# A two-stage graph network on one core: where the edge lists stand in SyncE's queue, and at which block of the first tile they are turned

## The reference, cut to what matters

```python
x = _layernorm(x + L0_gnn(x, edge_index, edge_type_2, ...))     # R-GCN, 2 relations, D_FF 286
x = _layernorm(x + L1_gnn(x, edge_index, ...))                  # 3 residual graph layers, 256 wide

def L0_gnn(h, edge_index, edge_type, ln_w, W_rel, W_root, bias, wo):
    xn = ln_w * (h * rsqrt(mean(h**2) + 1e-6))
    out = xn @ W_root + bias
    for r in range(2):
        w = (edge_type == r)
        sums = segment_sum(xn[src] @ W_rel[r] * w[:, None], dst)
        out = out + sums / maximum(segment_sum(w, dst), 1.0)[:, None]
    return h + elu(out) @ wo
```

## Time and profile before

| what | value |
|---|---|
| median of 3 runs | 584.37 us (583.69 to 584.87) |
| the profiled execution's own time | 585.49 us |
| its span | 583.7 us (so 1.79 us lie around the span) |
| TensorE busy | 97% of the span |
| VectorE, ScalarE, GpSimd busy | 65%, 40%, 17% |
| mean granted TensorE clock | 0.991 |

### The profile page before, as it was taken

The page is one execution under the profiler, slowest core; times in us unless marked ns, Lnnn a source line. Parts: engine busy times, 40 slices in busy tenths (PEclk is TensorE's granted clock), DMA queues, the critical chain, the costliest instruction groups (busy, mean ns, idle before and its releaser), DMA issues.

```text
span 583.7 us, 8611 instructions
## 1 busy us (share of the span) xinstructions
PE 566.7 (97%) x2704; PEld 410.8 (70%) x2704; DVE 380.4 (65%) x980; ACT 231.7 (40%) x477; POOL 100.6 (17%) x80
## 2 busy tenths in 40 slices
PE   6999999999999999999999999999999999999992
PEld 3566666566578898987898888877868867455541
DVE  7599988888837898988512330028748667755455
ACT  5444455533224546463321221013223233366555
POOL 3000000000000000003164512302202230132230
PEclk8999999999999999999999999999999999999997
DMA  8500111111031121129300000600100100021123
GB/s 261 154 26 13 35 35 35 35 35 35 0 89 40 37 62 46 46 71 247 128 20 0 0 0 1 226 1 1 38 1 0 36 0 1 1 71 52 54 70 105
DMA packets 20961, 30.74 MB, mean 53 GB/s; under 512 B 5458, under 2 KB 15404, under 8 KB 20928
## 3 DMA queue, kind: packets, MB, share of 16 engines
q1 hardware_dynamic: 20512, 29.66, 17.1%
q10 hardware_dynamic: 416, 0.67, 0.4%
HBM read 25.20 MB, written 5.12 MB: 52 GB/s over the span
## 4 chain that ended last, share of the span: by engine, by line
PE 92%; DMA 3%; DVE 3%; ACT 1%; SPq 0%; issue 0%; DVEq 0%
PE banks L745 20%; PE banks L949 12%; PE banks L1035 12%; PE banks L868 10%; PE banks L731 5%; PE banks L836 5%; PE banks L971 4%; PE banks L961 4%; PE banks L897 4%; PE banks L899 4%; PE banks L878 3%; PE banks L1025 3%; PE banks L739 1%; PE banks L853 1%; DMA w_all<-in_L_gnn_W_rel 1%; DMA cb_b<-in_L_gnn_conv_bias 1%
## 5 line engine op out<-in xcount | busy, mean ns | idle before, releaser
L745 PE MATMUL banks<-w_all,xnT 128*125 128x429 f32 x320 | 130.4, 532 | 2.3 <-DMA w_all<-in_L_gnn_W_rel 2.3
L745 PEld LDWEIGHTS banks<-w_all,xnT 128*125 128x125 f32 x320 | 54.6, 190 | 32.5 <-issue 29.7
L1198 DVE TENSOR_TENSOR adj<-adj,banks 125x220 f32 x160 | 60.9, 381 | 19.5 <-PE banks L731 17.4
L868 PE MATMUL banks<-hT,w_s 128*128 128x250 f32 x320 | 69.0, 375 | 0.2
L868 PEld LDWEIGHTS banks<-hT,w_s 128*128 128x128 f32 x320 | 60.2, 189 | 8.8 <-issue 1.4
L897 PE MATMUL banks<-y_hi,adj 125*125 125x288 f32 x200 | 55.2, 304 | 0.4 <-issue 0.4
L731 PEld LDWEIGHTS banks<-oh_code,oh_low 125*128 125x128 bf16 x320 | 31.0, 97 | 32.0 <-issue 27.9
L899 PE MATMUL banks<-y_lo,adj 125*125 125x286 f32 x200 | 53.5, 294 | 0.0
L1180 DVE TENSOR_TENSOR oh_code<-iota_c,edge 125x880 bf16<-125x880 f16 x80 | 48.9, 611 | 0.0
L1342 DVE TENSOR_SCALAR hT<-banks,g_c,b_c 128x125 f32<-128x125 f32 x60 | 19.4, 401 | 45.0 <-PE banks L853 45.0
L949 PE MATMUL banks<-adj,h_hi 125*128 125x250 f32 (+1 forms) x180 | 48.3, 367 | 0.1
(11 more groups left out here) (206 smaller groups left out, 896.8 us busy)
## 6 DMA issues: line engine op xcount, KB each, us to landing
xt<-in_x SPq DMA_DIRECT2D x15, 448.0 KB
out_x<-ot SPq DMA_DIRECT2D x9, 448.0 KB
w_s<-in_L_gnn_W SPq DMA_DIRECT2D x5, 512.0 KB, 6.4
xn<-in_x SPq DMA_DIRECT2D x5, 448.0 KB
wd_s<-in_L_gnn_Wd SPq DMA_DIRECT2D x1, 2048.0 KB, 12.1
w_all<-in_L_gnn_W_rel SPq DMA_DIRECT2D x6, 286.0 KB, 6.8
wo_s<-in_L_gnn_wo_weight SPq DMA_DIRECT2D x1, 1024.0 KB, 6.2
w_all<-in_L_gnn_W_root SPq DMA_DIRECT2D x3, 286.0 KB, 6.4
```

Source lines behind the costliest of these rows:

```text
L745: ins = pe.matmul(pb[0:P, 2 + 2 * v + n, 0:FH], xnT[:, u], w_all[:, u, n * FH:(n + 1) * FH], start=(u == 0), stop=(u == KD - 1))
L868: ins = pe.matmul(pb[:, b0 if f == 0 else 4 + f % 2, 0:2 * P], w1_s[:, k, f * 128:(f + 1) * 128], hT[:, k], start=(k == 0), stop=(k == KD ...
L1198: dve.tensor_tensor(cols, cols, window(b, q), ALU.add).then_inc(done, 1)
```

## The change

The three edge-list DMAs leave ScalarE's program and are issued by SP, behind w2 (which ends with the fourth eighth of the weights) and ahead of w3. The bounds are turned in front of block 4 instead of 2, the lows in front of block 5 instead of 4, the codes in front of block 6 instead of 5. Each of the first tile's eight blocks now adds one to a new semaphore, `first_turned`, as ScalarE copies it, and block u on TensorE waits for u + 1 of them. One of the two later warming products goes. `xnT_copied` is raised by two more at the start, so its later counts stay as they were.

```diff
--- before.py
+++ after.py
@@ -231,6 +231,7 @@
             sem(n) for n in ("o_gain", "o_res", "f_sq", "f_mv", "f_sd", "f_rstd", "f_shift", "f_done",
                              "xo_done"))
         tails_set = sem("tails_set")
+        first_turned = sem("first_turned")
         half_done, out_half = sem("half_done"), sem("out_half")
         half_mm, half_res, half_mean, half_sq, half_bias = (sem(n) for n in ("half_mm", "half_res", "half_mean", "half_sq",
                                                                             "half_bias"))
@@ -272,7 +273,12 @@
 
             load_x(0, 0)
             sp.dma_start(lnw8[:], ln_w.rearrange("(k p) -> k p", p=128)).then_inc(lnw_in, 16)
-            for q in range(len(PIECES)):
+            load_w(sp, 0)
+            load_w(sp, 1)
+            load_w(sp, 2)
+            for a, d, done in ((dst_i, dst, dst_in), (src_i, src, src_in), (typ_i, typ, typ_in)):
+                sp.dma_start(a[:], d.rearrange("(g e) -> g e", g=G)).then_inc(done, 16)
+            for q in range(3, len(PIECES)):
                 load_w(sp, q)
             load_x(1, 1)
             with sp.Fori(0, T // 2 - 1) as i:
@@ -418,7 +424,7 @@
 
         @block.scalar
         def _(act):
-            for s in (xnT_copied, y_copied, hT_lo, r1_done, d1_done):
+            for s in (xnT_copied, xnT_copied, xnT_copied, y_copied, hT_lo, r1_done, d1_done):
                 act.sem_inc(s, 1)
             def filled(r, cols, n):
 
@@ -476,15 +482,13 @@
 
             act.wait_ge(small_set, 1)
             act.activation(small1[:, 6:7], eps0[:, 0:1], ACT.Sqrt)
-            for a, d, done in ((dst_i, dst, dst_in), (src_i, src, src_in), (typ_i, typ, typ_in)):
-                act.dma_start(a[:], d.rearrange("(g e) -> g e", g=G)).then_inc(done, 16)
             act.wait_ge(lnw_ps, 1)
             act.copy(lnw[:], pb[:, 4, 480:480 + KD]).then_inc(lnw_set, 1)
             act.wait_ge(lnw_set, 1)
-            act.wait_ge(xnT_ps, 1)
-            weigh(0)
-            act.wait_ge(xnT_ps, 2)
-            weigh(1)
+            for k in range(KD):
+                act.wait_ge(xnT_ps, 1 + k // 4)
+                act.activation(xnT[:, k], pb[:, 6 + k // 4, k % 4 * P:(k % 4 + 1) * P], ACT.Copy,
+                               scale=lnw[:, k:k + 1]).then_inc(first_turned, 1)
             squares(0, 0)
             root_of(0, 0)
             act.wait_ge(small_set, 3)
@@ -785,24 +789,21 @@
             pe.wait_ge(xs_in[0], 32)
             turn(0, 0)
             turn(1, 0)
-            warm(2, 5)
+            warm(1, 5)
             for u in range(KD):
-                if u == 0:
-                    pe.wait_ge(xnT_copied, 1 + 1)
-                if u == 4:
-                    pe.wait_ge(xnT_copied, 1 + 2)
+                pe.wait_ge(first_turned, u + 1)
                 for q, ks in enumerate(PIECES):
                     if u == ks[0]:
                         pe.wait_ge(w_in[q], 48)
-                if u == 2:
+                if u == 4:
                     pe.wait_ge(bounds_ready, 1)
                     for i in range(2 * H):
                         ins = pe.transpose(pb[0:1, 4 + i // H, i % H * G:(i % H + 1) * G], bounds[:, i:i + 1], ident[0:G, 0:G])
                     ins.then_inc(bounds_ps, 1)
-                if u == 4:
+                if u == 5:
                     pe.wait_ge(lows_ready, 1)
                     turn_edges(0, e_low)
-                if u == 5:
+                if u == 6:
                     pe.wait_ge(edges_ready, 1)
                     turn_edges(1, e_code).then_inc(edges_ps, 1)
                 if u == KD - 1:
```

## The result

The changed kernel took 585.63 us (median of 12 executions, 584.69 to 587.77) against 584.71 us for the kernel before beside it (12 executions, 583.53 to 586.15). The ratio is 1.0024 with a 95% interval of 1.0013 to 1.0036. (The ratios are estimates of their own, with these intervals, and differ a little from the ratio of the two medians, here 1.0016.) I had forecast 582.4 and a gain.

What follows compares the result with a forecast made beforehand. TensorE was taken as bound by its 2.29 us wait for w0 and the low clock behind it. Row 0 at 21.95, 2.45 us sooner, less 0.45 gave 2.0 us: 582.4 us, range 581.3 to 584.2.

Steps and rivals of the forecast that it cites:

- the mixture: Median time: executions whose clock does not fall gain only 1.07 us, so 0.45 was taken off, leaving 2.0 us.
- the sum's 21.95: Start of row 0 on TensorE: w3 at 14.50 plus 7.45 us, 2.45 us sooner than 24.40.
- The step on the clock itself: TensorE's first blocks: granted clock 1.0 through 9 to 13 us; 1.70 us of work had been lost.
- my 7.4: Landing of w0, the first weights, without the edge lists' 1.73 us ahead; bounds 9.17 and 7.0.
- The rival by which w0 does not move: Start: w0 still lands near 9.2, the clock falls the same, time 584.4 us; chance 0.08.
- w3, the term that failed: Weights' piece awaited before the bounds are turned: lands at 14.50, between 14.20 and 15.06, instead of 15.06.
- the recovery: DMA engines in 5 to 8.5 us: 358 instead of 271 GB/s, at most 0.85 us; two thirds, 0.56, taken.
- The sum by the Trainium skill's rule: DMA queues: moving issues wins order, no bandwidth, so w3 stays at 15.06 and row 0 gains 1.89 us.
- What came behind w3: TensorE from w3's landing to row 0, all at the full clock: 7.45 us.
- What row 0 gains the end gains: Behind row 0: same order, transfers issued on engine events, so row 0's 2.45 us gain reaches the end.
- The later fall of the clock: Blocks 4 and 5: after short waits the clock falls later, row 0 at 23.65, time 583.6 us; chance 0.15.
- The late edge lists: VectorE's edge lists: landing too late, row 0 at 28.0, 3.6 later, time 588.0 us; chance 0.07.

Runs made afterwards that it cites:

- e1: The kernel before, unchanged, timed beside itself: 584.06 us, ratio 1.0001.
- e7: The changed kernel with the edge lists behind tile 1 in SP's queue, to look at landings only: 591.98 us, a single execution.
- e6: The changed kernel with the three edge DMAs issued by ScalarE, late, behind the norm's weight: 585.21 us, ratio 1.0013.
- e5: The kernel before with three idle SP instructions (raising a semaphore nobody reads) between w2 and w3: 585.76 us, ratio 1.0021.
- e9: The kernel before with three idle SP instructions behind w1's fourth part (w1 here L1's first weights): 583.77 us, ratio 0.9997.
- e13: The kernel before with three idle SP instructions where SP waits for adj_done: 585.33 us, ratio 1.0017.
- e14: The kernel before with 128 idle SP instructions where SP waits for adj_done: 584.33 us, ratio 0.9995.
- e10: The changed kernel with twelve idle SP instructions ahead of its wait for adj_done: 585.37 us, ratio 1.0022.
- e2: The changed kernel once more, no edit, against the kernel before: 585.98 us, ratio 1.0025.
- e8: The changed kernel with SP issuing w1's third and fourth parts only once the last tile's x has landed: 585.23 us, ratio 1.0014.
- e11: The changed kernel with 125 idle SP instructions ahead of its wait for adj_done: 584.65 us, ratio 1.0015.
- e4: The changed kernel with the edge DMAs back in ACT's queue, so only TensorE's order, block signals and one warming product less: 585.32 us, ratio 1.0008.

## Why the prediction was wrong

**The reference point.** The prediction summed against one execution with row 0 at 24.40, in which the clock had fallen. Without the fall row 0 is 22.89 (e1). I had reckoned 23.02 for such executions, which was near, and then took 0.45 us off for the mixture; the median of before lies so near e1's time that most of 1.4 (24.40 - 23.02) belonged there. That alone would have left a gain of about 1 us. What turned it are the next two steps that failed: from e1's 22.89 the sum's 21.95 is 0.94 sooner, w3 gave back 1.28 (15.78 instead of 14.50), what lies behind w3 another 0.24, and the end 1.02, which makes the 1.60 above. The step on the clock itself was right: at 7.29 the first block follows straight behind the warming product, and the clock stays at 1.00 where the earlier trace rows have 0.50.

**w0.** It landed at 2.86 + 3.4 = 6.26 by the DMA view, sooner than my 7.4 and than the lower bound of 7.0; the first block started at 7.29 against 7.55. The rival by which w0 does not move is refuted. Signalling the first tile's blocks one by one let block 0 start some 0.3 us sooner, since ScalarE copies them from 6.51 on at 0.27 us each and has four at 7.59; the wait of 1.45 us for w2 hid that, so it gained nothing, as costed.

**w3, the term that failed.** I bounded its landing by 14.20 and 15.06, on the step "the same bytes lie ahead of it after the change, so only the recovery moves it". It was 15.78, 0.7 outside. The recovery showed in 5 to 8.5 us (315 GB/s against 271) and was more than lost behind it (305 against 358): in 5 to 16 us the engines moved 3.4 MB instead of 3.6. The same bytes cost more late among the weights than early: against e7, which has none ahead, 2.15 us instead of 1.43, with 232 GB/s in 10 to 12 us where the earlier trace rows have 358. By e6 this holds in ACT's queue too. Why they cost more there stays open; that rows of 2000 and of 1144 bytes are mixed is a guess which no run separates. The sum by the Trainium skill's rule (DMA: Bandwidth & Descriptors, Rules for kernel authors: no bandwidth from spreading, only issue time) was nearer with 15.06, but it too had w3 no later than before, and no run here bears that out. What came behind w3 was sized well: 23.47 - 15.78 = 7.69 against my 7.45. Against e1 the change therefore loses 0.58 us up to row 0.

**"What row 0 gains the end gains".** This step failed as well. The order behind row 0 is the same, but SP's program is three instructions longer, and the last tile's x, needed 247 us later with hardly a margin, is about a microsecond late (1.02 us between row 0 and the residual). e5, e9, e13 and e14 show that the count of SP's instructions in front of that load is what matters; how the count reaches x, by the packet or otherwise, they do not show. I had weighed the three DMAs' issue time, and not that they are instructions.

**The rivals.** The later fall of the clock is real, and the changed kernel's own profile does not have it: e10's profiled execution has it, with row 0 at 27.04. Of the 59 executions with this start (changed, e2, e8, e10, e11), 13 have a mean clock of 0.991 or less, the lower bound used above, against 17 of 113 before. In the profiles the clock fell behind blocks 0 and 1 only after one long wait for w2 (3.61 us in e10, 2.60 in e6), and not after short waits as I had named: 1.45 and 0.97 in the changed kernel, 1.76 and 0.91 in e8, left the clock at 1.00. The late edge lists did not decide: `dst` landed at 6.25 + 6.2 = 12.45, VectorE began at 12.46 (I had said 11), and TensorE did not wait for it. None of my rivals had w3 later than before, or a loss behind row 0; the outcome was outside of my range.

**The account.** The start alone (e11) is 1.0015 (1.0006 to 1.0024), and the shifted instructions alone (e13) 1.0017 (1.0003 to 1.0032). Their sum, 1.0032, is compatible with the whole, 1.0024 (1.0013 to 1.0036), but each interval is wider than the difference, so the shares are not settled. Between the profiled executions of e1 and the changed kernel it is 0.58 and 1.02 us, 1.60 or 0.27%.

**Left open.** Why w2 lands at 11.65 in the changed kernel, a little before that in e11 and at 13.39 in e10, three kernels with the same start, I can't say. Nor is it separated whether the packet itself slows x, or SP's issues behind its fetch (a gap of some 0.2 us), or w1's third part that follows at once; e8 says that the last is a part of it. e10, whose x is in time and which still has 1.0022, leaves the size of x's share uncertain, as does e5, whose median lost more than its profile shows.

## What to carry to other kernels

Look at several executions before a start with a clock step in it is taken as typical; here one of 585.49 us was read where the median is 584.0. Before counting an edit to a DMA-issuing engine's program as only its issue time, look for transfers far behind it that land with under a microsecond to spare, and for the instruction queue's packets beside them: idle instructions can move them either way. And bytes that move to a later place among other loads do not keep their price, so a load behind them needs a margin for it.

## What the runs showed of the hardware

A packet of the instruction queue next to a tight load went with 0.4 to 1.1 us of delay (the residual 247.10 us behind row 0 in e5 and 247.78 in e13, against 246.68 in e9 and 246.65 in e14). The Trainium skill (DMA: Bandwidth & Descriptors, Queues, rings and completion order) calls row 14 of the queues the runtime's own, with refills in it; the traces agree as far as their q14 holds only packets of kind "instruction" (15 of them in the changed kernel). What such a packet does to a neighbour's landing is shown by these runs alone.

The edge rows among the weights' cost w3 as much as if they ran at 219 GB/s (changed kernel against e7), and the engines moved 299 to 305 GB/s in 8.5 to 16 us with them there (e6, changed kernel), against 355 without (e7). And with the same program the clock at the start fell or not from one execution to the next: in the kernel before's profile it did, in e1's it did not. The length of TensorE's wait for w0 does not tell them apart by itself: the clock fell behind 2.29 us (before), 2.13 (e4) and 1.96 (e13), not behind 1.01 (e1, e9) and 1.33 (e5), and in e14, by the products' time, behind 0.62.
